# Four chained layers: pooling as 32-row tiles over four banks, x1 early, keys ahead of the low product, new end and prologue

## The reference

```
x = x + L0(x)   tanh scorer per token, softmax over the row under a prefix, postfix or cloze mask by row type,
                pooled = p @ x / count
x = x + L1(x)   16 heads of 8, bias or gathered keys by row (u_prev decides); out @ Wo.T + bo
x = x + L2(x)   relu FFN 128 -> 512 -> 128 with common and per-row expert rank-16 corrections (8 experts)
x = x + L3(x)   gelu FFN 128 -> 512; 96 outputs shared, 32 by the row's expert (16 experts)
```

## Time and profile before

| | us |
|---|---|
| three runs | 280.24, 278.01, 279.27 |
| median | 279.27 |
| profiled execution, its own time | 279.37 |
| its span | 277.4 |
| TensorE busy, share of the span | 256.0, 92% |
| VectorE busy | 191.3, 69% |
| ScalarE busy | 139.5, 50% |
| GpSimd busy | 121.5, 44% |

### The profile page before, as it was taken

How to read it: one execution, slowest core, us unless ns; L and a number is a source line. 1 busy time by engine, 2 the same in 40 slices (tenths; PEclk the granted TensorE clock), 3 DMA queues, 4 the chain that set the end, 5 groups by cost and what they waited for, 6 DMA issues and landing times.

```text
span 277.4 us, 12601 instructions
## 1 busy us (share of the span) xinstructions
PE 256.0 (92%) x4845; PEld 187.0 (67%) x4845; DVE 191.3 (69%) x333; ACT 139.5 (50%) x257; POOL 121.5 (44%) x242
## 2 busy tenths in 40 slices
PE   7799998789999999999999999999999999889985
PEld 4565454567587867776677768676878587758854
DVE  4587746978878687887778687868786878371030
ACT  3463372186447635563746482756286438442240
POOL 2888313166506550554236433445154616461420
PEclk9996899999999999999999999999999999999999
DMA  7979101651255206530554045503553541255001
GB/s 203 358 214 272 35 2 59 229 209 45 58 213 217 91 2 235 213 116 0 191 218 159 0 151 209 206 0 113 197 220 129 212 156 40 85 223 192 2 0 40
DMA packets 26893, 38.25 MB, mean 138 GB/s; under 512 B 10721, under 2 KB 10977, under 8 KB 26738
## 3 DMA queue, kind: packets, MB, share of 16 engines
q1 hardware_dynamic: 26146, 36.99, 37.1%
q10 hardware_dynamic: 720, 0.89, 1.1%
HBM read 10.60 MB, written 2.10 MB: 46 GB/s over the span
## 4 chain that ended last, share of the span: by engine, by line
PE 38%; issue 19%; POOL 13%; POOLq 10%; DVE 9%; ACT 7%; DMA 1%; SPq 0%; ACTq 0%; DVEq 0%
POOLq L384 6%; PE pB L836 5%; PE pB L754 4%; POOL sc L366 4%; PE pB L708 3%; PE pB L712 3%; POOLq L394 3%; PE pS L683 3%; PE pB L789 2%; PE pB L709 2%; PE pA L645 2%; PE pA L651 2%; ACT L521 2%; POOL rw L385 2%; POOL x3b L374 2%
## 5 line engine op out<-in xcount | busy, mean ns | idle before, releaser
L385 POOL COPY rw<-e3t_s 128x128 f32 x128 | 39.4, 310 | 51.8 <-issue 45.6
L366 POOL TENSOR_TENSOR sc<-sc,rmax 128x512 f32<-128x512 f32 x32 | 33.5, 1049 | 57.5 <-DVE rmax L1101 57.4
L489 ACT ACTIVATE ex<-sc 128x512 f32<-128x512 f32 x32 | 20.2, 630 | 33.0 <-POOL sc L366 32.8
L836 PE MATMUL pB<-rw,hT 128*32 128x128 f32 x1024 | 31.8, 274 | 1.0 <-ACT hT L497 1.0
L754 PE MATMUL pB<-rwo,hT 128*32 128x128 f32 x1024 | 29.6, 273 | 2.1 <-ACT hT L493 2.1
L754 PEld LDWEIGHTS pB<-rwo,hT 128*32 128x32 f32 x1024 | 27.6, 110 | 3.2 <-issue 1.9
L836 PEld LDWEIGHTS pB<-rw,hT 128*32 128x32 f32 x1024 | 27.2, 110 | 3.3 <-issue 2.7
L1096 DVE SCALAR_TENSOR_TENSOR sc<-pS,bias 128x512 f32<-128x512 f32 x32 | 21.7, 677 | 11.1 <-PE pS L683 11.1
L1107 DVE STREAM_TRANSPOSE pt<-ex 128x512 f32<-128x512 f32 x32 | 22.6, 706 | 9.3 <-ACT ex L489 9.2
L395 POOL COPY rwo<-weff 128x512 f32 x32 | 21.5, 677 | 12.3 <-POOL x3b L374 5.5
L493 ACT ACTIVATE hT<-pB 128x512 f32<-128x512 f32 x32 | 18.3, 595 | 16.3 <-PE pB L712 16.1
(11 more groups left out here) (166 smaller groups left out, 517.2 us busy)
## 6 DMA issues: line engine op xcount, KB each, us to landing
rwo<-weff SPq DMA_DIRECT2D x96, 256.0 KB, 2.3
rw<-fc2t_dram SPq DMA_DIRECT2D x4, 768.0 KB, 12.7
out_dram<-o_s SPq DMA_DIRECT2D x8, 256.0 KB, 2.3
xT<-xt_dram SPq DMA_DIRECT2D x7, 256.0 KB, 2.6
xN<-xn_dram SPq DMA_DIRECT2D x7, 256.0 KB, 2.9
e3t_s<-e3t_dram SPq DMA_DIRECT2D x1, 1024.0 KB, 10.6
rwo<-ffn_w_dram SPq DMA_DIRECT2D x1, 896.0 KB, 6.4
rwo<-ffn_w_dram SPq DMA_DIRECT2D x1, 512.0 KB, 12.1
```

The lines of the kernel that those rows point to most:

```text
L366: pool.tensor_tensor(sc[:, g % 2, :, :], sc[:, g % 2, :, :], rmax[:, g % 2, :].unsqueeze(2).to_broadcast([P, H, S]), ALU.subtract).then_in ...
L385: pool.tensor_copy(rw[:, r, :, SHARED:D], e3t_s[:, bass.ds(e, 1), :, :].rearrange("p o c n -> p (o c) n"))\
L836: last = mm(pB2[S * q:S * q + S, P * g:P * g + P], hT[:, c, tok], rw[:, Q4 * g + q, c, :], start=(c == 0), stop=(c == FC - 1))
```

## The change

Pooling takes each row of 32 tokens as a tile of 32 array rows; the four row slots q go to four banks (pA0, pA1, pS0, pS1, now one tensor `pooled`). The spread copies and poolP are gone. TensorE issues pooling of the next block ahead of `out_rows`, VectorE makes its weights ahead of the second `turn` and x1 of the next block ahead of the second `normalise`. x1 plus the output bias is kept in a tile x1b of its own, made by ScalarE, so that x2 is a plain sum. In a step TensorE does queries and keys ahead of `low`, VectorE `keys` ahead of `mask_low`. `out_rows` goes to two banks, group by group between the weighings, and is copied out in two halves. `hid` and hT are separate buffers; btmp shares space with x3b and x3n. The end interleaves block 6's `final` groups with block 7's layers and runs block 7's last product chunk by chunk over four banks, stored in four pieces. The prologue has another order on each engine.

```diff
+        pooled = ctx.enter_context(nc.psum_tensor("pooled", [P, Q4, 512], F32))
+        pA0, pA1, pS0, pS1 = (pooled[:, q, :] for q in range(Q4))
+        OUT = [pB2, pB1]
...
             def pooling(i):
                 at(pe, ld_xN, 16 * (i + 1))
-                at(pe, spread_sb, Q4 * (i + 1))
+                at(pe, l0_step, L0_STEPS * (i + 1))
                 at(pe, k_sb, i)
+                at(pe, sc_sb, G * i)
                 for g in range(G):
-                    last = mm(pA0[:, P * g:P * g + P], xN[:, g, :], poolP[:, g, :], start=True, stop=True)
+                    for q in range(Q4):
+                        k = slice(S * q, S * q + S)
+                        last = mm(pooled[:, q, S * g:S * g + S], xN[k, g, :], poolT[k, g, :], start=True, stop=True)
...
+            def biased_x1(i):
+                at(act, x1_sb, i + 1)
+                at(act, x2_sb, i)
+                act.activation(x1b[:, :], x1T[:, :], ACT.Identity, bias=bo_eff[:, 0:1]).then_inc(x1b_sb, 1)
...
             def out_rows(i):
-                at(act, out_ps, G * (i + 1))
-                act.activation(outn[:, :, :].rearrange("p g d -> p (g d)"), pB2[:, :], ACT.Copy).then_inc(outn_sb, 1)
+                for half in range(2):
+                    k = slice(2 * P * half, 2 * P * half + 2 * P)
+                    at(act, out_ps, G * i + 2 * half + 2)
+                    act.activation(lowm[:, k], OUT[half][:, k], ACT.Copy).then_inc(outn_sb, 1)
...
-            store(NBLK - 1)
+            for g in range(G):
+                sp.wait_ge(end_sb, g + 1)
+                sp.dma_start(out[NBLK - 1, :, g, :], o_s[:, g, :]).then_inc(st_out, 16)
...
-            def token_major(i):
+            def token_major(i, ps=pB0):
                 at(pe, x3b_sb, i + 1)
-                at(pe, low_sb, 2 * NBLK if isinstance(i, int) and i == NBLK - 1 else 2 * (i + 2) - 1)
+                if not (isinstance(i, int) and i >= NBLK - 2):
+                    at(pe, low_sb, 2 * (i + 2) - 1)
...
@@ TensorE, step_of @@
+                queries(n)
+                keys(n)
                 if last is None:
                     pe.wait_ge(weff_sb, 2 * Q4)
                     pe.wait_ge(w_low, 1)
                 low(n - 1)
-                queries(n)
-                keys(n)
                 if last is not None:
                     token_major(last)
...
                 hidden_expert(n - 1, 3)
-                weigh(n, 2)
-                out_rows(n - 1)
-                weigh(n, 3)
                 if next_block:
                     pooling(n + 1)
+                out_rows(n - 1, 0, 1)
+                weigh(n, 2)
+                out_rows(n - 1, 2)
+                weigh(n, 3)
+                out_rows(n - 1, 3)
                 out_turn(n - 1)
                 attn_out(n)
                 fc1(n - 1)
@@ TensorE, the end @@
             low(NBLK - 1)
-            token_major(NBLK - 2)
-            for g in range(G):
-                final(NBLK - 2, g)
+            final(NBLK - 2, 0, pA0)
+            final(NBLK - 2, 1, pA0)
             for c in range(FC):
                 hidden(NBLK - 1, c)
                 hidden_expert(NBLK - 1, c)
-            keep_busy(2, pA0, ffn_p[0])
-            out_rows(NBLK - 1)
-            keep_busy(3, pA0, ffn_p[0])
+            final(NBLK - 2, 2, pA0)
+            out_rows(NBLK - 1, *range(G))
+            final(NBLK - 2, 3, pA0)
             out_turn(NBLK - 1)
-            keep_busy(4, pA0, ffn_p[0])
+            token_major(NBLK - 2, pA1)
+            keep_busy(2, pS0, ffn_p[0])
             fc1(NBLK - 1)
-            token_major(NBLK - 1)
-            for g in range(G):
-                final(NBLK - 1, g)
+            token_major(NBLK - 1, pB0)
+            final_by_chunk(NBLK - 1)
@@ VectorE, step_of @@
+                keys(n)
                 mask_low(n - 1)
-                keys(n)
...
                 score_max(n, 2)
+                if next_block:
+                    pool_weights(n + 1, 1)
                 turn(n, 1)
                 score_max(n, 3)
                 turn(n, 2)
                 normalise(n, 0)
-                if next_block:
-                    pool_weights(n + 1, 1)
                 turn(n, 3)
+                if next_block:
+                    x1(n + 1)
                 normalise(n, 1)
                 x3(n - 1)
                 x2(n)
-                if next_block:
-                    x1(n + 1)
@@ ScalarE, step_of @@
                 queries(n)
+                biased_x1(n)
                 table(n, ACT.Exp)
...
-                if next_block:
-                    spread_weights(n + 1)
                 out_rows(n - 1)
...
+            LAST = [pV, pA1, pA0, pB1]
+            def final_by_chunk(i):
+                at(pe, rw_sb, ROWS * (i + 1))
+                at(pe, x3n_sb, i)
+                at(pe, res_sb, i)
+                for c in range(FC):
+                    at(pe, g_sb, FC * i + c + 1)
+                    for g in range(G):
+                        for q in range(Q4):
+                            tok = slice(P * g + S * q, P * g + S * q + S)
+                            last = mm(LAST[g][S * q:S * q + S, 0:P], hT[:, c, tok],
+                                      rw[:, Q4 * g + q, c, :], start=(c == 0), stop=(c == FC - 1))
+                        if c == FC - 1:
+                            last.then_inc(end_ps, 1)
@@ TensorE, prologue @@
             keep_busy(14, pS0, x2p[0])
             pooling(0)
-            keep_busy(2, pS0, x2p[0])
+            keep_busy(2, pV, x2p[0])
...
-            keep_busy(2, pS0, x2p[0])
+            keep_busy(3, pS0, x2p[0])
             scores(0, 0)
+            keep_busy(3, pA0, x2p[0])
             prepare_wi()
             prepare_last_bias()
             keep_busy(4, pA0, x2p[0])
             scores(0, 1)
+            keep_busy(3, pA0, x2p[0])
             base_out(0, 0)
...
             weigh(0, 1)
             base_out(1, 0)
-            base_out(1, 1)
+            pe.wait_ge(weff_sb, 2)
+            pooling(1)
             weigh(0, 2)
             base_out(1, 2)
+            weigh(0, 3)
             base_out(1, 3)
+            base_out(1, 1)
+            attn_out(0)
             pairs_out(1)
-            pe.wait_ge(weff_sb, 2)
-            pooling(1)
-            weigh(0, 3)
-            pe.wait_ge(w_high, 1)
-            keep_busy(5, pA1, ffn_p[0])
-            attn_out(0)
-            keep_busy(4, pA1, ffn_p[0])
@@ GpSimd, prologue @@
+            values_home()
             scorer_blocks()
             indices()
             strength()
-            pool.memset(vb[:, :, :, :, :], 0.0).then_inc(prep_pool, 1)
...
-            expert_ids()
+            third_layer_ids()
+            second_layer_ids()
```

More of the change, by code:

```diff
@@ L379, in expert_weights @@
             def expert_weights(i, part):
-                if part == 0:
+                if isinstance(i, int) and i == NBLK - 1:
+                    pool.wait_ge(row_ps, part + 1)
+                elif part == 0:
                     at(pool, fin_ps, i + 1)
@@ L561, in _ @@
             exps(0, 2)
+            act.wait_ge(prep, P_FBIAS)
+            biased_x1(0)
             l0_exps(1)
@@ L744, in hidden_expert, with out_rows @@
                 parts3(HID[c][:, :], weight(N_EIB, c), whole(lowp), False, True, (lowl_sb, i + 1)).then_inc(hid_ps, 1)
-            def out_rows(i):
-                at(pe, hid_sb, FC * (i + 1))
-                for g in range(G):
+            def out_rows(i, *groups):
+                if groups[0] == 0:
+                    at(pe, hid_sb, FC * (i + 1))
+                for g in groups:
+                    ps = OUT[g // 2]
                     at(pe, rwo_sb[g], 16 * len(DMA_ROWS) // G * (i + 1))
@@ L819, in fc1, with token_major, final @@
                 parts3(GIN[FC - 1][:, :], weight(N_FC1, FC - 1), whole(x3p), True, True).then_inc(g_ps, 1)
-            def token_major(i):
+            def token_major(i, ps=pB0):
                 at(pe, x3b_sb, i + 1)
-                at(pe, low_sb, 2 * NBLK if isinstance(i, int) and i == NBLK - 1 else 2 * (i + 2) - 1)
+                if not (isinstance(i, int) and i >= NBLK - 2):
+                    at(pe, low_sb, 2 * (i + 2) - 1)
                 for g in range(G):
-                    last = pe.transpose(pB0[:, P * g:P * g + P], x3b[:, P * g:P * g + P], ident[:, :])
+                    last = pe.transpose(ps[:, P * g:P * g + P], x3b[:, P * g:P * g + P], ident[:, :])
                 last.then_inc(x3t_ps, 1)
-            def final(i, g):
+            def final(i, g, ps=pB2):
                 if g == 0:
@@ L835, in final @@
                         tok = slice(P * g + S * q, P * g + S * q + S)
-                        last = mm(pB2[S * q:S * q + S, P * g:P * g + P], hT[:, c, tok],
+                        last = mm(ps[S * q:S * q + S, P * g:P * g + P], hT[:, c, tok],
                                   rw[:, Q4 * g + q, c, :], start=(c == 0), stop=(c == FC - 1))
-                if g == G - 1:
+                if ps is not pB2:
```

(17 more changed lines are left out.)

103 lines of the change are left out of this document (54 added, 49 removed).

## The result

The changed kernel takes **294.08 us** (median of four executions, 294.02 to 295.18); the kernel before takes 279.61 beside it (278.01 to 280.24). The ratio is 1.055, with a 95% interval of 1.052 to 1.058. Slower was forecast at 0.67; 284.5 us and the range to 293.0 were both too low.

A forecast was written before the change was run, and what follows sets the result against it. TensorE's program plus its waits was taken to bound each step (28.00 of 29.20 us busy). Loop +10.0, step 7 +1.75, prologue and step 1 -3.7, end -2.9 sum to +5.15: 284.5 us, range 275.5 to 293.

The forecast's parts named there:

- the mechanism of the step: Loop step up to scores: TensorE's transposes wait some 2.5 us for lowm, behind VectorE's kb; scores start 2.06 us later.
- pooling: Pooling in 32 records on 32-row tiles: 1.0 us from start to start, no difference from before.
- the end: End of the kernel, with final groups interleaved and the last product done in chunks: -2.9 us.
- the prologue: Prologue and step 1: -3.7 us with the clock at 2.4 GHz, -1.7 if it falls as before.
- Clock 1.00 in 23 to 30 us: A sign to look for: full TensorE clock in that stretch of the prologue.
- the clock falls in the hole: Rival: TensorE drops to half rate in its wait for lowm, +15 if in each of six steps; chance 0.12.
- every second one: Within the clock rival: a half-rate stretch in every second of six steps, +7 us.
- the wait at +0.4: Step 1: hidden_expert waits for kb and the low mask in one, +0.4 us.
- the second half of a step: Loop step from the scores on: waits gone and waits added give -0.45 to +0.2 us, taken as 0 less 0.05.
- the second weighing: Second half of a loop step: it waits for VectorE's second turn, later by 0.25 to 0.9 us.
- The waits that went: Second half of a loop step: four TensorE waits disappear, giving back 1.2 us, 0.40 of it at pooling.
- step 7: Shorter last step: +2.3 for the wait for lowm, -0.55 as attention output no longer waits, +1.75 us in all.

The follow-up runs named there:

- e1: The changed kernel with VectorE's mask_low put back ahead of keys in every step; 283.82 us, ratio 1.008.
- e3: The changed kernel with token_major moved behind scorer_out in TensorE's step; 277.41 us, ratio 0.995.
- e4: The kernel before with only VectorE's keys put ahead of mask_low; 310.99 us, ratio 1.113.
- f3: e3 with the pooling products of blocks 2 to 7 issued twice; 284.13 us, ratio 1.016.
- g3: e3 with the end of the kernel before, on all engines; 282.69 us.
- f2: e3 with VectorE's second turn put back ahead of pool_weights part 1; 274.13 us, ratio 0.981.
- g2_clock_only: The changed kernel, waits and orders kept, with filler products in the idle places of steps 1 to 7 and the prologue; 287.87 us, ratio 1.028.
- f4: e3 with the next block's queries put ahead of out_turn and its keys ahead of fc1; 280.28 us, ratio 1.003.
- e2: The changed kernel with nine filler products between the low product and the transposes in steps 2 to 7; 294.0 us, ratio 1.044.
- f1: e3 with filler products in step 1's two TensorE waits; 278.97 us, ratio 0.983.

## Why the prediction was wrong

**Right: the mechanism of the step.** The transposes' wait names `lowm`, 2.35 against 2.5 forecast; up to the scores the step grows by 2.06, the very number, in which 0.15 too much hole happens to cancel against 0.1 too little work ahead of it and 0.06 behind it. kb starts right behind the keys (139.22, where the wait names the keys). e1, e3 and e4 each show by another way that VectorE's order together with pB0's guard makes it.

**Right: pooling.** 1.02 from start to start, 0.91 by doubling, against 1.0. The rule of the Trainium skill (TensorE: Matmul & The Clock Gate, LDWEIGHTS) that a load's time goes by its columns gives 3.4 as an estimate, if the loads go one after another. They do not: f3 and the load records show them over each other.

**Right: the end and the prologue at full clock.** The end is worth 2.7 (g3) or 3.24 (from `low` of block 7 to the end of the span, 27.17 against 30.41), against 2.9, and the last product starts 3.16 earlier after that `low`, against 3.15. To the transposes of step 2 the table has -1.5 against -1.6 once the clock holds. Clock 1.00 in 23 to 30 us came too.

**Wrong: the clock was a rival and not a term.** This is the step that failed: my sum put half rate in the loop and in step 1 at nothing. I gave 0.12 to "the clock falls in the hole", arguing that idle stretches of up to 1.1 us had kept it in the loop and none of 2.5 was shown. The reading was wrong too: the loop steps before have no idle stretch of TensorE over 0.35 us; the 1.1 stands in step 1. And the absence of a long one was no evidence for the full clock. The runs show a fall in three of six holes, which is the "every second one" of that rival: +7 there, because I priced a fall at 2.5, and 4.9 here (17.4 less 12.5), 1.6 to 1.7 each. The fall in step 1 I had not written at all: I noted that `hidden_expert` would wait for kb and the low mask, costed the wait at +0.4, and looked only at the prologue for the clock. Its 10.2 us at half rate cost 1.9 (the first line of the table, +0.5 against -1.5). With 0.3 behind the loop that is 7.2 between the profiled spans and 6.2 between the medians, out of the 9.6 us that I was off.

**Mis-sized: the second half of a step.** Taken as 0 less 0.05; measured +0.21 (22.43 from scores to queries, against 22.22). Of its parts, the second weighing was 0.71 later, where I had 0.25 to 0.9 and took a middle: the collision did happen (multiply 0.90 beside GpSimd's subtraction), and f2 shows its place, collision included, worth 0.66. `out_turn` cost +0.41 against 0.5. The waits that went gave back 0.9 and not 1.2: I had 0.40 for pooling's wait, where the row says 0.30, and the idle times in the trace, 0.26, 0.30, 0.15 and 0.28 less the 0.22 that stayed, add up to 0.8. So a step of 31.47 against 31.2. In the five steps of the table +12.5 stands against +10.2. Of this 1.35 is the longer step; 0.6 comes because two steps of the kernel before were shorter than 29.2, and 0.5 because step 2 is now longer (31.93 in `g2_clock_only`). These make 0.2 too much, which the forecast had added for step 7's hole.

**Mis-sized: step 7.** From its transposes to `low` of block 7, -0.55 was forecast and +1.37 measured (26.34 against 24.97); in `g2_clock_only` it is +1.0. Three waits of TensorE, two of them with nothing that the profile names, make most of it:

```profile
244.68 0.40 PE L705 MATMUL pooled<-kb,qT 32*32 32x128 f32 x2 [0.34 <-issue]
255.85 1.95 PE L778 MATMUL pB<-rwo,hid 128*32 128x128 f32 x64 [0.69 <-ACT hid L511]
260.68 0.42 PE L778 MATMUL pB<-rwo,hid 128*32 128x128 f32 x6 [0.48 <-issue]
```

The 0.69 is the relu's wait: in the loop pooling covers it, and step 7 has no pooling. I had counted the loop's cover where it is missing.

**Open.** Why the clock fell in steps 2, 4 and 6 and not in 3, 5 and 7 behind the same hole, and why the prologue falls in some executions of one kernel: no run separates it. It is no rule of every second step: behind the longer holes of e4 the clock fell in steps 2, 3, 4, 6 and 7, and one of the changed kernel's own four executions has, by its mean clock of 0.971 against 0.965, some 3.5 us less at half rate than the others. The wait in front of `out_turn` (the half copy of the bank) was not tried by itself.

## What to carry to other kernels

Before two operations of one queue change places, look up whose guard names the one that goes back, on every engine, and what stands behind that guard: here one exchange on VectorE held up TensorE's whole queue, and moving the waiter behind work that was ready gave it back (a step of 29.31 in e3 against 29.20 before). Price each new wait of TensorE twice, by its length and by work at half rate behind it, in the prologue and the written-out steps too. And before filling a wait, look what it was covering on the other engines: f4 gained two waits and got two longer ones.

## What the runs showed of the hardware

- Stretches at 1.2 GHz lasted 3.4 us in the loop (changed kernel, e4), 6.8 in the prologue of the kernel before and of f3, 10.2 in step 1 and in the prologue of e4, and 13.7 in the prologue of e1, e2, f1 and f4. Idle stretches of 0.82 and 1.57 us, 4 us apart, stood before one of 10.2 us in five profiles and before none in two; 2.34 to 2.44 us of idling stood before one of 3.4 in three steps of the changed kernel and before none in three.
- A stretch at half rate cost half its length in the loop (3.4 us of it 1.6 to 1.7), and far less in step 1 (10.2 us of it 1.9). Together 20.5 us cost the changed kernel 6.2.
- VectorE's multiply of two 128x128 SBUF tensors took 0.29, with GpSimd's 128x512 subtraction done (f2), and 0.90 beside it (e3 and the changed kernel).
- 16 products on 32-row tiles with loads of 128 columns, over four banks, took 0.91 to 1.02 us in 32 records, as long as 8 records of 128-row tiles (1.0).
